# A four-layer MetaFormer on one core: when VectorE, GpSimd and the route transposes do their preparation steps

## The reference, cut to what matters

```python
x = x + L0_conv(ln_c(x));  t = t + L0_ffn(ln_t(t))   # 1x1 convs, softmax map, 3x3 convs; sinkhorn routing, 8 experts
x = x + L1_conv(ln_c(x));  t = t + L1_ffn(ln_t(t))   # per-image 7x7 filters; top-2 mixture, silu, 128-512-128
x = x + L2_conv(ln_c(x));  t = t + L2_ffn(ln_t(t))   # offsets and a gate per image; top-2 mixture, gelu, 128-512-128
x = x + L3_conv(ln_c(x));  t = t + L3_ffn(ln_t(t))   # saliency from pooled x; top-2 mixture, relu, 128-256-128
# a mixture, for every expert e (all tokens go through all experts):
h = act(xt @ W1[e] + b1[e]);  out = out + (h @ W2[e] + b2[e]) * score[:, e:e + 1]
```

## Time and profile before

| | |
|---|---|
| runs | 449.14, 449.72, 454.06 us |
| the profiled execution | 454.66 us, span 452.9 us |
| PE busy | 402.8 us, 89% of the span |
| ACT, DVE busy | 281.8 us (62%), 269.6 us (60%) |
| POOL busy | 159.7 us (35%) |
| mean granted PE clock | 0.95 |
| 103 to 160 us | filters |
| 160 to 453 us | mixtures: block 0 to 219, 1 to 276, 2 to 334, 3 to 391, 4 to 424, 5 to the end |

### The profile page before, as it was taken

How to read it: one execution, slowest core, us unless ns; L and a number is a source line. 1 busy time by engine, 2 the same in 40 slices (tenths; PEclk the granted TensorE clock), 3 DMA queues, 4 the chain that set the end, 5 groups by cost and what they waited for, 6 DMA issues and landing times.

```text
span 452.9 us, 4966 instructions
## 1 busy us (share of the span) xinstructions
PE 402.8 (89%) x1601; PEld 285.4 (63%) x1603; DVE 269.6 (60%) x559; ACT 281.8 (62%) x504; POOL 159.7 (35%) x130
## 2 busy tenths in 40 slices
PE   6998979888799989999999859999799995979893
PEld 2466647543555668887777647776577673757672
DVE  0634135785343278566496684585856849475865
ACT  4231134764110377777796956997959987588682
POOL 4800000367970001322567645122124553332243
PEclk9979997999669989999999989999999999889998
DMA  8920000000017003211010004034031100311051
GB/s 297 420 74 0 0 0 2 1 0 1 0 46 326 0 1 106 82 49 48 30 40 25 0 1 118 24 79 154 0 103 39 46 2 0 117 47 25 2 170 63
DMA packets 10673, 28.75 MB, mean 63 GB/s; under 512 B 1079, under 2 KB 2231, under 8 KB 10392
## 3 DMA queue, kind: packets, MB, share of 16 engines
q1 hardware_dynamic: 10648, 28.43, 18.4%
HBM read 27.81 MB, written 0.62 MB: 63 GB/s over the span
## 4 chain that ended last, share of the span: by engine, by line
PE 48%; ACT 27%; DVE 17%; issue 4%; DMA 2%; POOLq 0%; SPq 0%; ACTq 0%; DVEq 0%; POOL 0%
PE ps L393 10%; PE ps L395 9%; PE ps L394 9%; ACT hidh L908 9%; ACT ps L909 8%; PE ps L400 3%; PE ps L570 2%; DVE hidl L1216 2%; ACT rstd L819 2%; PE ps L624 2%; ACT rstd L821 2%; PE ps L405 2%; PE ps L453 1%; DVE bot L1138 1%; ACT L957 1%
## 5 line engine op out<-in xcount | busy, mean ns | idle before, releaser
L1216 DVE TENSOR_TENSOR hidl<-ps,hidh 128x512 fp32r<-128x512 f32 x160 | 107.7, 688 | 65.0 <-ACT ps L909 64.8
L367 POOL TENSOR_TENSOR x<-x,parts 128x512 f32<-128x512 f32 x47 | 61.0, 1297 | 208.0 <-DVE parts L1226 113.1
L908 ACT ACTIVATE hidh<-ps,par 128x512 fp32r<-128x512 f32 x96 | 68.1, 710 | 31.5 <-PE ps L395 31.4
L393 PE MATMUL ps<-xh,wh_all 128*128 128x512 f32 x160 | 69.7, 436 | 5.6 <-DVE hidl L1216 3.3
L393 PE MATMUL ps<-hidh,wh_all 128*128 128x512 f32 (+1 forms) x162 | 69.1, 427 | 2.7 <-DVE hidl L1216 2.5
L909 ACT ACTIVATE ps<-ps,par 128x512 f32<-128x512 f32 x96 | 65.8, 685 | 0.0
L394 PE MATMUL ps<-hidh,wl_all 128*128 128x512 f32 (+1 forms) x162 | 64.0, 395 | 0.0
L395 PE MATMUL ps<-hidl,wh_all 128*128 128x512 f32 (+1 forms) x162 | 64.0, 395 | 0.0
L395 PE MATMUL ps<-xl,wh_all 128*128 128x512 f32 x160 | 64.0, 400 | 0.0
L394 PE MATMUL ps<-xh,wl_all 128*128 128x512 f32 x160 | 63.8, 399 | 0.0
L360 POOL TENSOR_TENSOR wl_all<-wa,wh_all 128x512 fp32r<-128x512 f32 x40 | 51.2, 1298 | 3.5
(11 more groups left out here) (228 smaller groups left out, 605.9 us busy)
## 6 DMA issues: line engine op xcount, KB each, us to landing
scores_all<-rows_scratch SPq DMA_DIRECT2D x48, 256.0 KB, 3.4
wa<-in_moe SPq DMA_DIRECT2D x2, 4096.0 KB, 15.5
wa<-in_moe SPq DMA_DIRECT2D x1, 2048.0 KB, 9.7
dft_x<-in_dft_x SPq DMA_DIRECT2D x1, 640.0 KB
dft_o<-in_dft_o SPq DMA_DIRECT2D x1, 640.0 KB
w<-in_w_bottom SPq DMA_DIRECT2D x1, 576.0 KB, 6.7
w<-in_w_out SPq DMA_DIRECT2D x1, 576.0 KB, 8.4
cst<-in_consts SPq DMA_DIRECT2D x1, 512.5 KB, 7.5
```

The costliest lines, as they stand in the source:

```text
L367: pool.tensor_tensor(half(x, h), half(x, h), parts[:, n % 2, :], ALU.add).then_inc(s["state_added"], 1)
L393: pe.matmul(o, wh, xhi, start=start, stop=False)
L908: act.activation(hidh[:, n % 2, f, :], sums, func, bias=bias).then_inc(s["hidden_hi_act"], 1)
L1216: dve.tensor_tensor(hidl[:, n % 2, f, :], bank(sums_bank(n, f)), f32(hidh[:, n % 2, f, :]), ALU.subtract).then_inc(s["hidden_lo"], 1)
```

## The change

It moves steps and trades one rounding per unit between engines; what is computed stays.

- One chunk per unit of units 9 to 39 (chunk 2 of the wide, 1 of the narrow) is rounded into `hidh` by DVE, from PSUM, instead of by ACT.
- DVE's preparation steps are spread over the gaps between chunks: pooled sums and offset or saliency inputs after low(.,0) and low(.,1) of the third unit, `norm_low` and `route_start` after the first two chunks of the seventh, `route_end` after the first chunk of the next block.
- The transposes of the routes of blocks 2 to 4 come after the second `front` of their own block, in one transpose of 32 columns instead of four of 8; `keep_rows` follows there, and the first `scale` of the block is put off until after the next unit's chunks. The row store and spread DMAs take the new shape.
- POOL splits four experts after the filters' activation and four in block 0; moe2's load moves behind seven score spreads.
- In the start, transposes, sums and mixing go between the taps; four dummy matmuls are put ahead of the first convolution.
- ACT: high parts before the silu table load, `high_part` one chunk later, exp instead of tanh for layer 3's routes.

```diff
+        def rounds_on_dve(n, f):
+            return E < n < 5 * E and f == (2 if n < WIDE else 1)
...
+                    if n == E - 1:
+                        sp.wait_ge(s["w_split"], E)
+                        sp.dma_start(wa[:], dram["moe2"]).then_inc(s["moe2_loaded"], 16)
+                    sp.dma_start(scores_all[:, slot, :].rearrange("c (t p) -> c t p", p=C),
+                                 dram["rows"][m, 4 * h:4 * h + 4, e * C:(e + 1) * C].unsqueeze(0)
+                                 .to_broadcast([C, 4, C])).then_inc(s[f"scores{slot}_in"], 16)
...
-            sp.wait_ge(s["w_split"], E)
-            sp.dma_start(wa[:], dram["moe2"]).then_inc(s["moe2_loaded"], 16)
...
-            x_ready(pool, 2, 1)
+            pool.wait_ge(s["filt_act"], 1)
             pool.wait_ge(s["moe1_loaded"], 16)
-            for e in range(E):
+            for e in range(EARLY):
                 split_expert(e, 1024)
+            pool.wait_ge(s["norm_lo"], 6)
             for n in range(E):
+                for e in range(EARLY + 2 * n, min(EARLY + 2 * n + 2, E)):
+                    split_expert(e, 1024)
                 add_part(n)
...
+
+            keep_clock(4, 7)
             pe.wait_ge(s["wb_split"], 1)
             conv33(0, xph, xpl, s["norm_hi"], s["norm_lo"], 0, s["bottom_done"],
-                   between={**{(0, 3 + b): lambda b=b: scores(b) for b in range(B)}, (1, 0): turn_max, (1, 1): spread_max})
...
+                   between={**{(0, 4 + b): lambda b=b: scores(b) for b in range(B)}, (1, 0): turn_max, (1, 1): spread_max,
+                            (1, 3): lambda: turn_bottom(0), (1, 5): lambda: sum_exp(0), (1, 6): lambda: mix(0)})
...
-                   between={(1, 2): lambda: center(1, 0), (1, 4): lambda: variance(1, 0)})
+                   between={(0, 2): lambda: turn_bottom(1), (0, 3): lambda: sum_exp(1), (0, 4): lambda: mix(1),
+                            (1, 2): lambda: center(1, 0), (1, 4): lambda: variance(1, 0)})
...
-                    last = pe.transpose(bank(6, E, C, t * C), wgt[:, (4 * h + t) * E:(4 * h + t + 1) * E], ident)
-                last.then_inc(s["route_turned"], 1)
+                pe.transpose(bank(6 if kb < 2 else 7, WIDE, C), wgt[:, WIDE * h:WIDE * (h + 1)], ident).then_inc(s["route_turned"], 1)
...
@@ -748,6 +766,8 @@
                 for j in range(E):
                     front(kb * E + j + 1)
                     if j == 0:
+                        if kb >= 2:
+                            turn_route(kb)
...
+                        if kb >= 2:
+                            pe.wait_ge(s["rows_ready"], kb + 1)
                         variance(4, hh)
                     elif j == 2:
...
-                act.activation(hidh[:, n % 2, f, :], sums, func, bias=bias).then_inc(s["hidden_hi_act"], 1)
+                if not rounds_on_dve(n, f):
+                    act.activation(hidh[:, n % 2, f, :], sums, func, bias=bias).then_inc(s["hidden_hi_act"], 1)
                 act.activation(sums, sums, func, bias=bias).then_inc(s["hidden"], 1)
+
...
-            act.preload_act_table_set("silu_and_others")
             for h in range(2):
                 high_part(3, h)
+            act.preload_act_table_set("silu_and_others")
             for n in range(E + 1):
...
-                            if j == 6:
-                                high_part(5, hh)
+                        elif (j, f) == (7, 0):
+                            high_part(5, hh)
...
-                        elif (j, f) == (7, 3):
+                        elif (j, f) == (7, 3) and kb == 1:
+                            act.preload_act_table_set("gelu_and_others")
+                        elif (j, f) == (8, 0):
                             route_tanh(kb + 1)
-                            act.preload_act_table_set("gelu_and_others")
...
-                    if (j, f) == (1, 1):
+                    if (j, f) == (0, 0):
+                        route_exp(4)
...
+            def pool_sums(n, h):
                 dve.wait_ge(s["normed"], seq(n, h))
+                step(dve.tensor_reduce(pool4[:, 2 * h:2 * h + 2], half(xn, h).rearrange("p (b n) -> p b n", b=2), AX.X, ALU.add))
+
...
             def low(n, f):
-                dve.wait_ge(s["hidden_hi_act"], chunks(n) + f + 1)
                 dve.wait_ge(s["hidden"], chunks(n) + f + 1)
+                if rounds_on_dve(n, f):
+                    step(dve.tensor_copy(hidh[:, n % 2, f, :], bank(sums_bank(n, f))))
+                else:
+                    dve.wait_ge(s["hidden_hi_act"], hi_by_act(n, f))
                 dve.tensor_tensor(hidl[:, n % 2, f, :], bank(sums_bank(n, f)), f32(hidh[:, n % 2, f, :]),
...
-                step(dve.tensor_scalar(seg(rem, h), seg(ew, h), -1.0, 1.0, ALU.mult, ALU.add))
-                step(dve.reciprocal(seg(oh2, h), seg(rem, h)))
-                step(dve.scalar_tensor_tensor(seg(ew, h), seg(ew, h), 1.0, seg(oh2, h), ALU.add, ALU.mult))
+                if MOE[m]["layer"] != 3:
+                    step(dve.tensor_scalar(seg(rem, h), seg(ew, h), -1.0, 1.0, ALU.mult, ALU.add))
+                    step(dve.reciprocal(seg(oh2, h), seg(rem, h)))
+                    step(dve.scalar_tensor_tensor(seg(ew, h), seg(ew, h), 1.0, seg(oh2, h), ALU.add, ALU.mult))
...
                     n = kb * E + j
                     for f in range(4):
                         low(n, f)
-                        if (j, f) == (5, 2):
+                        if (j, f) == (1, 1) and kb == 2:
+                            keep_rows(2)
+                        elif (j, f) == (3, 0):
+                            pool_sums(4, hh)
+                        elif (j, f) == (3, 1):
+                            offset_inputs(hh)
+                        elif (j, f) == (5, 2):
                             gate_half(hh)
-                        elif (j, f) == (8, 2):
-                            keep_rows(kb + 1)
-                    scale(n - 1)
+                        elif (j, f) == (7, 0):
+                            norm_low(5, hh, 4 + nx + 1)
+                        elif (j, f) == (7, 1):
+                            route_start(nx)
+                        elif (j, f) == (8, 0):
+                            route_end(nx)
+                    if j == 2 and kb == 2:
+                        scale(n - 2)
+                    if j > 1 or kb == 1:
+                        scale(n - 1)
                     if j == 2:
-                        offset_inputs(hh)
+                        norm_half(4, hh)
                     elif j == 3:
                         positions(hh)
                     elif j == 6:
                         norm_half(5, hh)
-                        norm_low(5, hh, 4 + kb + 2)
-                        route_start(kb + 1)
-                        route_pick(kb + 1)
                     elif j == 7:
-                        route_end(kb + 1)
+                        route_pick(nx)
...
                     low(n, f)
-                    if (j, f) == (4, 0):
+                    if (j, f) == (1, 0):
+                        keep_rows(4)
+                    elif (j, f) == (3, 1):
+                        threshold(1)
+                    elif (j, f) == (4, 0):
                         saliency_half(1)
-                scale(n - 1)
                 if j == 2:
+                    scale(n - 2)
+                if j > 1:
+                    scale(n - 1)
+                if j == 2:
+                    norm_half(6, 1)
+                    pool_sums(6, 1)
                     saliency_inputs(1)
-                elif j == 3:
```

More of the change, by code:

```diff
@@ new lines, in sum_exp, with mix @@
+            def sum_exp(h):
+                pe.wait_ge(s["exp_done"], 2 * h + 2)
+                pe.matmul(bank(2 * h, cols=2), k("ones"), es[:, 2 * h:2 * h + 2], start=True, stop=True).then_inc(s["exp_summed"], 1)
+            def mix(h):
+                pe.wait_ge(s["bottom_ready"], h + 1)
+                for b in (2 * h, 2 * h + 1):
+                    for par_ in range(2):
+                        for j in range(2):
+                            last = pe.matmul(bank(6 + h, cols=C, first=(b % 2) * PIX + par_ * C),
+                                             expo[:, b, j, par_::2], bot_t[:, 2 * b + j, :], start=(j == 0), stop=(j == 1))
+                    last.then_inc(s["mixed"], 1)
@@ L860, in _, with mix_high @@
                                accum_out=es[:, b:b + 1]).then_inc(s["exp_done"], 1)
-            bottom_bias(1)
-            for h in range(2):
+            def mix_high(h):
                 act.wait_ge(s["mix_added"], 2 * h + 2)
```

171 lines of the change are left out of this document (90 added, 81 removed).

## The result

The changed kernel took 438.23 to 441.74 us in four runs, median **439.75**, against 451.89 for the kernel before beside it: ratio 0.971, 95% interval 0.965 to 0.977. Timed again with the experiments it took 438.21 against 454.73: 0.964 (0.957 to 0.971). Some executions of every kernel run over 1.5% slower than its fastest, at a lower clock; medians and ratios here leave them out, the full-clock times further down do not. The forecast was 438, the range 430 to 446; against 449.72, the median of before that it started from, that is -11.7, and against the kernel beside it the measured change is -12.1. The profiled execution took 441.74 us against 454.66 of before: -12.9.

A forecast was written before the change was run, and what follows sets the result against it. PE bounds steady units, so only its gaps can be won. Terms sum to -13.5 us: 441.2 from the profiled 454.66, 436.2 from the median 449.72; forecast 438, this case 432 to 444, 8-in-10 range 430 to 446.

The forecast's parts named there:

- Filters: Filters: POOL's splits moved off DVE's tiny steps -3.6, two later steps -0.3, half clock -1.5; mixtures' start: table load -1.3.
- rival B: Clock stays up in the filters and at all edges: 12 us instead of about 4.5, giving 431; chance 0.2.
- Start: Around the convolutions: 1.9 us of gaps shrink, dummy matmuls and switches cost as much; net 0, bounds -2 and +1.5.
- Block 0: Start of the mixtures: POOL's splits of two experts slow block 0's tiny routing steps, +1.2 us.
- Rounding on DVE: Mixture units: one copy out of PSUM moves from ACT to DVE in 31 units, hidden by PE in steady units; 0.
- Rival C: DVE's copies out of PSUM are blocked by POOL, 31 units losing 0.7 us, giving 460; chance 0.05.
- Middles: Middles of blocks 1 to 3: offsets and saliency wait for two chunks of the third unit; +2.1 us (0.2, 0.7, 1.2).
- Edges: Block edges 1-2, 2-3, 3-4: route transpose leaves the path, chunks are late next; -2.0, -0.5, -4.8, together -7.3 us.
- Rival A: Edges end where they did; only the filters gain 5.4 and block 4 gains 1, giving 443 to 448; chance 0.22.
- Block 4: Block 4: shorter chain to the 2.35 us wait -1.1, its half clock -1.5, later scores +0.5; -2.1 us.
- End: End of the kernel: three routing steps gone, smaller row copy, one copy more; -0.7 us.
- pieces: Score spreads in pieces of 512 bytes, not 2048: +0.3 us inside block 4's +0.5, bounds 0 and +1.5 per block.

The follow-up runs named there:

- splits back: Changed kernel with all eight of POOL's first-mixture weight splits back in their old place beside VectorE's small filter steps; 446.5 us, ratio 0.979 to the kernel before.
- splits only: Kernel before with only POOL's part as changed and the second mixture's load behind seven of block 0's spreads; 449.6 us, ratio 0.983 to the kernel before.
- five edits: Changed kernel with rounding on ACT, 2048-byte score pieces, offset/saliency inputs together, six splits before block 0, routing's end in three pieces; 427.7 us, 0.939 to before.
- long pieces: Changed kernel with route rows stored expert by expert, so a spread reads one piece of 2048 bytes; 436.3 us, ratio 0.956 to the kernel before.

## Why the prediction was right, and where it was wrong

- **Filters (-5.4 with the clock; -1.3 for the table load).** Waits: right, 3.6 us gone, undone by *splits back*. The table load gave 1.35. The clock was mis-sized: 1.5 taken, 6.1 measured as the remainder of the 9.7. I took the lower end because the small matmuls stayed; with PE's gap ahead of them gone they ran at full clock in ten of twelve profiles. In this stretch rival B (6.8 us) was nearly right. Not settled: why the other two (*splits only* and *five edits*) still have 6.8 us of half clock there, with no wait over 1.31 us ahead of it.
- **Start (0).** It was worth 1.3 to 1.6 us in the traces at equal clock, 2.1 in full-clock time. The gaps shrank as counted, the dummies and switches cost next to nothing: the first convolution started behind a 0.53 us wait for its weights, which covered the dummies. In the profiled execution 3.4 us more of half clock (10.2 against 6.8) hid the gain.
- **Block 0 (+1.2).** +1.9, by the mechanism named: steps of 0.5 to 0.7 us beside splits 4 and 5. Both profiles have one stretch of half clock there.
- **Rounding on DVE (0).** Units stayed at 5.56 us, subtractions at 0.687. Rival C is out.
- **Middles (+2.1).** +2.4, with waits where predicted (0.83, 1.53, 2.57 us).
- **Edges (-7.3).** -2.9, -1.0, -4.5. The center of block 4 waited 1.10 us for POOL's addition and started 0.1 behind it, as forecast. The -4.8 of the third edge was read off at "near 386"; the working ahead of it, 385.0 + 1.29, gives -4.4. At the edge 1 to 2 the wait of 4.34 became one of 2.73 for `hidl`. Rival A is out: the edges did not end where they did. VectorE was the late engine in block 4.
- **Block 4 (-2.1, of which -0.6 in this stretch).** The step that failed: +1.4. I took the 2.35 us wait's chain and made it shorter, but looked at nothing else that VectorE does there: the new order puts the scores' store and both scalings ahead of the saliency's inputs. VectorE's timeline: 

```profile
381.08 0.75 DVE L1267 SCALAR_TENSOR_TENSOR parts<-ps,par,scores_all 128x512 f32<-128x512 f32 x1 [0.54 <-DMA scores_all<-rows_scratch]
381.99 0.75 DVE L1267 SCALAR_TENSOR_TENSOR parts<-ps,par,scores_all 128x512 f32<-128x512 f32 x1 [0.16 <-DMA scores_all<-rows_scratch]
382.65 0.68 DVE L1076 TENSOR_TENSOR xn<-ps,rstd 128x512 f32<-128x512 f32 x1
...
384.67 0.42 DVE L1368 TENSOR_TENSOR spread<-small,par 128x256 f32<-128x256 f32 x1
```
 
  PE then waits 1.61 us for `spread`, for which it had waited 0.27, and still 1.62 for the center. With the routing as before the stretch takes 13.33 us, with all rounding on ACT 14.67.
- **End (-0.7) and pieces (+0.3), with block 4's -1.5 of clock.** +1.4. The half clock behind the center is gone, but as much of it stands behind the wait of 2.43 us at the start of block 5. The broadcast was mis-sized: 1.7 us more to landing, exposed at the starts of blocks 4 and 5; with long pieces the stretch takes 1.3 us less than before. The rule that I cited (the Trainium skill, "DMA: Bandwidth & Descriptors", Specifications: full line rate from 512 bytes) would have made it nothing; 5.1 us to landing against 3.3 is what the runs show here.

The total came out right by luck: 4.4 us too little in the filters stood against 5.5 too much in the mixtures. (The chance of faster by over 1%, put at 0.81, adds up to 0.79 from its parts.)

## What to carry to other kernels

Work of another engine that stands beside tiny steps on a critical chain is worth moving first: here it cost 3.6 us of waits, and then 6.1 us of clock behind PE's gap. A wait taken off one chain in an engine that works in order comes back as a wait for whatever was queued behind; count the whole queue of that engine up to the next thing PE needs, as was done at the edges and not in block 4. Where several transposes become one, look at what it does to the pieces of the DMA behind it: storing the rows in another order kept both gains.

## What the runs showed of the hardware

- A broadcast of 256 KB to 128 partitions takes 5.0 to 5.2 us to land from pieces of 512 bytes (eight kernels) and 3.3 to 3.4 from 2048 bytes (five).
- Small VectorE steps that work in SBUF alone take 0.17 to 0.22 us with POOL idle. Beside POOL's casts, subtractions and additions many of those with two inputs or with scalars (TENSOR_SCALAR) took 0.5 to 1.2: all 14 of over 0.45 us behind the start in the changed kernel ended 0.02 to 0.05 us behind an instruction of POOL. Reductions, maxima and reciprocals kept their time beside POOL (0.19, 0.17 and 0.17 to 0.36 us), and so did subtractions of 512 columns that read PSUM (0.69).
- Waits of 2.7 to 2.9 us at the edge 1 to 2 had a stretch of half clock right behind them in eight of the nine profiles that have them, while at the start the same kernel had 0 us of it in one profile and 10 in the other: one profile of a kernel can't price a term of the clock.
